# A two-layer graph network with norms: no GpSimd drain between stages, gathers eight groups ahead, and another order on three engines

## What is computed

```python
def L0(x, src, dst, ew):                       # first layer
    agg = segment_sum(x[src] * ew[:, None], dst, N)
    out = leaky(x * agg @ W1 + b1) + leaky(agg @ W2 + b2)     # slope 0.2
    return out * rsqrt(max(sum(out * out), 1e-12))
def L1(x, src, dst, ew):                       # second layer
    msg = ffn(x[dst], W1p, b1p, W2p, b2p) * ew[:, None]       # two products, a gelu after each
    agg = segment_sum(msg, src, N)
    out = ffn(concat([x, agg]), W1u, b1u, W2u, b2u)
    return out * rsqrt(max(sum(out * out), 1e-12))
x = layernorm(x + L0(x, src, dst, ew))
x = layernorm(x + L1(x, src, dst, ew))
```

## Time and profile before

| | |
|---|---|
| median of 3 runs | 2987.17 us (2985.78 to 2990.58) |
| the profiled execution, its own time | 3010.83 us |
| its span | 3009.1 us |
| mean granted TensorE clock | 0.798 of full speed |
| busy share of the span | TensorE 71%, VectorE 74%, ACT 35%, GpSimd 78% |
| first edge stage ends, second begins | 1290 us |
| second edge stage ends, last begins | 2610 us |
| DMA | 516.47 MB, mean 172 GB/s |

### The profile page before, as it was taken

One profiled execution on the slowest core, in us unless ns is written; L12 is line 12 of the kernel. 1 busy time (PEld: TensorE's weight loads), 2 busy tenths in 40 slices (PEclk: granted clock), 3 DMA queues, 4 the chain that ended last, 5 costly groups with the idle time before them and its releaser, 6 DMA issues. The chain is left out here.

```text
span 3009.1 us, 39225 instructions
## 1 busy us (share of the span) xinstructions
PE 2149.7 (71%) x11956; PEld 1675.8 (56%) x11956; DVE 2212.4 (74%) x5627; ACT 1059.1 (35%) x1964; POOL 2345.0 (78%) x1774
## 2 busy tenths in 40 slices
PE   2126655555555554249899899989999998699997
PEld 2025655454554544237666666666666666466664
DVE  2149998888888886437777777777777777288888
ACT  0000000000000000025555455555454554288887
POOL 7767788888888788736888888888888887488888
PEclk9995555555555555569999999999999999699998
DMA  9879888888888767447777777777777776356664
GB/s 224 201 152 200 197 181 175 173 180 180 183 175 172 154 142 153 79 137 168 178 178 171 175 169 177 177 177 177 176 172 175 174 171 138 83 194 206 210 205 157
DMA packets 1036086, 516.47 MB, mean 172 GB/s; under 512 B 540544, under 2 KB 998336, under 8 KB 1035880
## 3 DMA queue, kind: packets, MB, share of 16 engines
q1 hardware_dynamic: 764616, 372.57, 46.8%
q0 software_dynamic: 144256, 77.17, 19.1%
q10 hardware_dynamic: 127008, 64.23, 7.5%
HBM read 269.97 MB, written 243.84 MB: 171 GB/s over the span
## 5 line engine op out<-in xcount | busy, mean ns | idle before, releaser
L300 PE MATMUL sums<-xg,weigh 128*128 128x64 f32 x1960 | 439.5, 418 | 595.8 <-ACT ms L323 328.7
L300 PEld LDWEIGHTS sums<-xg,weigh 128*128 128x128 f32 x1960 | 425.1, 328 | 628.4 <-issue 524.3
L545 POOL DMA_INDIRECT state<-ms,sidx x392 | 635.8, 1622 | 174.5 <-issue 117.7
L256 POOL DMA_INDIRECT table<-ms,sidx x392 | 621.5, 1585 | 154.7 <-issue 127.0
L368 DVE TENSOR_SCALAR weigh<-rowp,key,ew 128x128 f32<-128x128 f32 (+3 forms) x784 | 424.1, 603 | 289.2 <-PE rowp L288 131.7
L531 POOL DMA_INDIRECT box<-table,node_dst x392 | 382.2, 975 | 128.4 <-issue 113.9
L243 POOL DMA_INDIRECT xg<-in_x,node_src x392 | 382.3, 975 | 120.8 <-issue 107.0
L323 ACT ACTIVATE ms<-sums 128x256 f32<-128x256 f32 x98 | 37.6, 383 | 1160.6 <-DMA table<-ms,sidx 860.1
L374 DVE SCALAR_TENSOR_TENSOR seen<-rowp,key,earlier 128x128 f32<-128x128 f32 (+3 forms) x784 | 383.4, 545 | 0.0
L578 PE MATMUL z_p<-turned_s,wz 128*128 128x512 f32 x588 | 331.7, 647 | 38.2 <-ACT turned_s L651 20.2
L588 PE MATMUL o_p<-cenz,leaky 128*128 128x65 f32 x2352 | 287.1, 279 | 31.0 <-issue 15.9
(11 more groups left out here) (94 smaller groups left out, 3539.2 us busy)
## 6 DMA issues: line engine op xcount, KB each, us to landing
box<-table SPq DMA_DIRECT2D x97, 768.0 KB
joins<-weigh ACTq DMA_DIRECT2D x98, 640.0 KB
weigh_in<-joins SPq DMA_DIRECT2D x98, 640.0 KB
table<-rows SPq DMA_DIRECT2D x97, 512.0 KB
pair<-state SPq DMA_DIRECT2D x97, 512.0 KB, 3.8
xin<-in_x SPq DMA_DIRECT2D x97, 256.0 KB
state<-y SPq DMA_DIRECT2D x97, 256.0 KB
out<-y SPq DMA_DIRECT2D x97, 256.0 KB, 2.2
```

What stands on the lines that cost most here:

```text
L256: pool.indirect_dma_start(out=table[:, :], out_offset=bass.IndirectOffsetOnAxis(ap=sidx[0][:, i:i + 1], axis=0), in_=ms[k % MR][:, b, :], ...
L300: last = pe.matmul(sums[k % 2][:, a * D:(a + 1) * D], block_of(0, k, b)[:, a * P:(a + 1) * P], xg[:, k * WT + b, :], start=b == a, stop=b ...
L545: pool.indirect_dma_start(out=state[:, :], out_offset=bass.IndirectOffsetOnAxis(ap=sidx[1][:, at:at + 1], axis=0), in_=ms[k % SM][:, b, :] ...
```

## The change

Four things. All three blocks are opened with no_gpsimd_drain=True. The second edge stage gathers LEAD = SB + 2 = 8 groups ahead instead of 6, with six box buffers as before, so that gathers 6 and 7 stand before scatter 0 on GpSimd's queue and wait for added 1 and 2. TensorE runs first_product before turn 0. ACT runs take and square_centred before neighbours_in, and first_gelu between evict 0 and evict 1. VectorE runs normalize before scale, and sum_centred before multiply.

```diff
-                with nc.Block() as block:
+                with nc.Block(no_gpsimd_drain=True) as block:
...
                 SB, SY, SW, SM = 6, 4, 3, 3
+                LEAD = SB + 2
...
-                        for i in range(SB):
+                        for i in range(LEAD):
                             for h in range(HALVES):
                                 gather(i, h)
                         for k in range(NWIN):
                             for h in range(HALVES):
                                 scatter(k, h)
-                                if k + SB < NWIN:
-                                    gather(k + SB, h)
+                                if k + LEAD < NWIN:
+                                    gather(k + LEAD, h)
...
                             of(t, 2, outputs, 1)
+                            of(t, 4, first_product)
                             of(t, 1, turn, 0)
-                            of(t, 4, first_product)
                             of(t, 1, turn, 1)
...
                             of(t, 5, second_gelu)
                             of(t, 2, slope, 2)
+                            of(t, 5, take)
+                            of(t, 3, square_centred)
                             of(t, 4, neighbours_in)
-                            of(t, 3, square_centred)
                             of(t, 2, square)
                             of(t, 1, evict, 0)
+                            of(t, 4, first_gelu)
                             of(t, 1, evict, 1)
                             of(t, 1, slope, 0)
-                            of(t, 5, take)
-                            of(t, 4, first_gelu)
                             of(t, 1, evict, 2)
                             of(t, 1, slope, 1)
...
                             of(t, 1, leak, 0)
+                            of(t, 3, normalize)
                             of(t, 2, scale)
-                            of(t, 3, normalize)
                             of(t, 1, leak, 1)
                             of(t, 2, add_rows)
                             of(t, 1, leak, 2)
+                            of(t, 2, sum_centred)
                             of(t, 0, multiply)
-                            of(t, 2, sum_centred)
```

## The result

The kernel after the change took 2977.95 us (median of 8 runs, 2972.03 to 2982.28); the kernel before, measured beside it, 2987.84 us (8 runs, 2984.17 to 2990.79). The ratio is 0.9968, 95% interval 0.9959 to 0.9977: 9.6 us less by the ratio (9.9 between the medians). Forecast were 17.4 less; the range held the time.

A forecast was written before the change was run, and what follows sets the result against it. GpSimd's queue of scatters and gathers was taken as the bound. Drains -11.9, earlier take -6.0 and the chain +0.5 (lead's gain against multiply's stalls) gave -17.4: 2970 us timed, range 2953 to 2986.

The forecast's parts named there:

- multiply's place: Second edge stage: VectorE's multiply holds up GpSimd starts, 0.23 us a round for 32 rounds, then 0.3 for 58.
- The drains: GpSimd drains at two block ends, 6.59 and 5.27 us, vanish with nothing in their place: 11.9 us gained.
- The rival that their time would turn up elsewhere: GpSimd may be finishing something at the first end: 2976 us, or 2982 if the flag changes nothing; chance 0.15.
- The take sooner: Start of the second edge stage: ACT's take follows TensorE's join directly, so the first scatter comes 6.0 us sooner.
- The sign that I had named: In the new profile, the first scatter comes about 70 us after the stage's first gather rather than 75.8.
- The lead: Gathers eight ahead: two more scatter groups run without gathers at the end, 9.53 instead of 12.83 us each; 6.6 us gained.
- the 58 locked rounds: Rounds after the first 32, when compute has used its three-buffer lead and each take waits for a landing; 0.3 us stall each.
- the picture of a multiply that slides evenly over the eight starts: First 32 rounds: compute runs free and multiply slides across eight GpSimd starts a round, costing 0.23 us a round.
- full collision: Rival: multiply stalls the fourth gather 0.85 us in every later round, 32 us more, 3002 us; chance 0.08.
- Multiply missing the gather: Rival: multiply starts clear of the fourth gather, 17.4 us of stalls go, sum -35, 2952 us; chance 0.14.
- The compute loop as the bound: Rival: the compute loop decides from above 12.9 us a round; 13.2 would add 27 us; about 12.0 expected; chance 0.04.
- Carrying the profile over to the timed runs: The -17.4 us from the 3010.83 us profiled execution is applied whole to the 2987.17 us timed median, giving 2970.

The follow-up runs named there:

- the first set: One chip: flag only, eight ahead only, new order only, and changed kernel with three-part multiply; before 2988.77 us. Its traces include the changed kernel's.
- the third set: One chip: changed kernel (ratio 0.9989), it with multiply before sum_centred (1.0041), multiply split (1.0009), split and six ahead (1.0036); before 3012.31 us.

## Why the prediction was right, and where it was off

The direction and the range were right, and each term can be found in the new profile, but the largest term in dispute, multiply's place, came out right in part by luck. In the first set's terms:

- **The drains**: 11.9 forecast, 11.8 measured in the pauses, 10.2 in the medians of the drains alone. The rival that their time would turn up elsewhere falls, and with it the stall for code that the Trainium skill's page "Runtime: NRT & Kernel Launch", Instruction fetch mechanics, could have put beneath them: no run here shows it at these two ends.
- **The take sooner**: 6.0 forecast, 4 to 6 measured against the old order in the same set. The take stands right behind the join. The sign that I had named, 70 us from first gather to first scatter, was wrong by 11: 58.5. Those 11 us lie between chips, not between kernels: in the profile of before ACT's first squares came late, and my steps were read from it.
- **The lead**: the run-off of eight groups was to take 73.9 us and takes 75.1. GpSimd's idle time in the opening is in two pieces (8.48 and 9.14 us), not three; the first of the two waits for added did not stop it. The pieces come to 17.6 us where 29 were forecast; the missing 11 are those of the item above.
- **Multiply's place**: this is the term that was mis-sized. In the words of the prediction, "8 x 0.85 / 12.64 x 0.43 = 0.23 us a round" for the first 32 rounds: measured 13.10 - 12.64 = 0.46. That is 7.3 us over 32 rounds. The 0.3 for the 58 locked rounds came to 0.335, 2 us. With 1.2 us in the run-off the chain is 10.5 us longer than the 1236.3 forecast. In the first rounds the picture of a multiply that slides evenly over the eight starts failed. Multiplies come 11.95 us apart. A stall makes GpSimd's round 13.2 to 13.5 us, so the next multiply falls 1.25 us or more earlier in GpSimd's order, and gathers start only 1.25 to 1.33 us apart: a multiply that has met one gather meets the one before it in the next round, at nearly the same offset. In the later rounds the sentence "Afterwards each take waits for a landing" failed. Of the 62 takes from round 28 to the end of the 90, 26 do, and the landings that hold them come after 1.7 us or after 3.4 to 5.1, not spread over 1.5 to 2.8. The stall is not 0.3 us in each round but about 1.2 (0.8 to 1.4) and 0.4 in two rounds of five. That this gives 0.335 on average, near my 0.3, is luck. All this is read from the trace; no experiment held the phase fixed.
- **The rivals**: full collision is refuted by the 0.335. Multiply missing the gather did not happen, but splitting it brought nearly that time by another way: 2957 measured, 2952 forecast for the rival. The compute loop as the bound had 4 in 100; it is not so on the chip that the result comes from, and it is so on the chip of the third set, where the change gains 0.1%, within 0 and 0.2. Its slack of "some 1.7 us" was read off a trace in which the loop waited for GpSimd, and a loop that waits does not show such a delay as a cost.
- **Carrying the profile over to the timed runs**: the prediction allowed that GpSimd might be 0.8% quicker in them. It was not, as the chain takes 1235.8 us in the slow profile and 1235.9 on the fast chip. The 23.7 us between the profiled and the timed before lie, by the first set's kernels, before the end of the first edge stage (some 13 us) and in the opening (some 11), so carrying the whole of -17.4 over was sound.

The sum: -17.4 with 10.5 more in the chain is -6.9, measured -9.6; the 2.7 us between them are within the spread of the runs (before's alone is 6.6 us wide), and what they consist of is not shown.

## What to carry to other kernels

Where GpSimd issues DMAs back to back and is the bound, look at a long VectorE instruction with both inputs in SBUF, as multiply here, as a stretch in which GpSimd may not get going, and cut it into shorter ones before moving it about: three parts took 20.7 us off on one chip, while another place for it took nothing off. It pays only while that queue is the bound. Gathering further ahead moves everything that GpSimd's queue meets: eight groups ahead alone cost 15 us, through late landings and collisions. And run the winner on another chip: a gain of 1.1% on one was no gain on the next.

## What the runs showed of the hardware that I had not expected

- A GpSimd DMA instruction issued during VectorE's two-input multiply was lengthened as if it could not begin until some 0.82 us after multiply had: losses of 0.71 us at an offset of 0.11 and 0.26 at 0.56, and 0.81 to 0.84 for offset plus loss in all 62 cases of the changed kernel. Cut into three, the largest loss is 0.26 us. The page "GPSIMD Engine Reference" of the Trainium skill, Key points, names the contention; the trace agrees and gives it a size.
- A GpSimd drain at the end of a block, after its last scatter, took 6.59 and 5.27 us, and leaving it out saved 11.8 us with nothing in its place.
- The landing of a scatter group took 1.7 us in some rounds and 3.4 to 5.1 in others of the changed kernel, and up to 7.0 with the lead alone.
- Chips differ in more than a factor. ACT's square started 0.04 us after the product it needed in the first set's traces and 0.2 to 1.1 us after it in the others (medians), with TensorE's granted clock much the same (0.94 to 1.00 against 0.92 to 1.00 in windows between 1400 and 2500 us). In the others ACT also had unexplained waits ("remote" in the profile): of up to 14.7 us in the stage's opening, and of up to 5 us later, 27 of them, 109.5 us, in one run of the third set. The first set's traces have none.
